# Rows of a two-product expert layer transposed by DMA instead of on TensorE

## The reference

```
x = x + tanh(g_xattn) * expert(layernorm(x), ids)     # every row has one of 4 experts, by its token id
      g = silu(h @ W_e^T); u = h @ W_e^T; y = (g * u) @ W_e   # W_e = ctx[e], 512 x 512, used three times
x = x + tanh(g_ffn) * ffn(layernorm(x))
      base (512 x 512) + shared LoRA + 6 routed LoRA experts (top 2 of a softmax), + bias
```

## Time and profile before

| | us |
|---|---|
| median of 3 runs | 231.8 |
| span of the profiled execution | 229.7 |
| TensorE matmul busy (PE) | 211.8 (92%) |
| TensorE weight load busy (PEld) | 181.7 (79%) |
| VectorE busy | 168.1 (73%) |
| GpSimd busy | 95.4 (42%) |
| ScalarE busy | 77.2 (34%) |

### The profile page before, as it was taken

How to read it: one execution, slowest core, us unless ns; L and a number is a source line. 1 busy time by engine, 2 the same in 40 slices (tenths; PEclk the granted TensorE clock), 3 DMA queues, 4 the chain that set the end, 5 groups by cost and what they waited for, 6 DMA issues and landing times.

```text
span 229.7 us, 4143 instructions
## 1 busy us (share of the span) xinstructions
PE 211.8 (92%) x1203; PEld 181.7 (79%) x1204; DVE 168.1 (73%) x423; ACT 77.2 (34%) x166; POOL 95.4 (42%) x147
## 2 busy tenths in 40 slices
PE   0666999999999999999999999999999999999990
PEld 0325788888888888888888889999999999999990
DVE  5878787777865666555566566768999989999761
ACT  4554334323422122222222216044333344333330
POOL 4887743332223333332100111116666665556742
PEclk9997999999999999999999999999999999999998
DMA  4986082111111111001100000001111111211122
GB/s 126 376 248 212 1 288 72 45 46 46 46 46 46 46 46 40 13 39 46 46 0 0 0 0 0 3 1 47 49 46 46 46 46 46 83 54 46 46 93 91
DMA packets 5994, 15.00 MB, mean 65 GB/s; under 512 B 1073, under 2 KB 1073, under 8 KB 5986
## 3 DMA queue, kind: packets, MB, share of 16 engines
q0 software_dynamic: 2800, 9.18, 12.4%
q1 hardware_dynamic: 2544, 4.21, 5.4%
q10 hardware_dynamic: 642, 1.52, 2.0%
HBM read 10.71 MB, written 4.19 MB: 65 GB/s over the span
## 4 chain that ended last, share of the span: by engine, by line
PE 75%; DVE 10%; issue 6%; POOL 5%; ACT 1%; DMA 1%; POOLq 1%; DVEq 0%
PE z_ps L466 17%; PE y_ps L466 17%; PE y_ps L471 8%; PE z_ps L471 8%; PE hT_ps L476 6%; PE ffn_b L466 4%; PE actT_ps L476 4%; PE ffn_a L466 3%; POOL xg L278 2%; PE ffn_b L471 2%; PE actT_ps L552 2%; DVE bn L845 2%; PE ffn_a L471 2%; POOL lo_onehot L294 2%; DVE hwT L893 1%
## 5 line engine op out<-in xcount | busy, mean ns | idle before, releaser
L269 POOL TENSOR_SCALAR var_eps<-stats 128x1 f32<-128x1 f32 x35 | 7.0, 201 | 107.6 <-DVE stats L757 107.4
L466 PE MATMUL z_ps<-ct_split,hT 128*128 x144 | 39.3, 417 | 1.2 <-ACT hT L349 1.2
L466 PE MATMUL y_ps<-ct_split,actT 128*128 x152 | 39.7, 403 | 0.0
L466 PEld LDWEIGHTS z_ps<-ct_split,hT 128*128 128x128 f32 x144 | 26.7, 195 | 6.5 <-issue 1.5
L466 PEld LDWEIGHTS y_ps<-ct_split,actT 128*128 128x128 f32 x152 | 27.2, 189 | 5.2 <-ACT actT L357 0.2
L357 ACT ACTIVATE actT<-actT_ps 128x512 fp32r<-128x512 f32 x19 | 11.4, 599 | 44.8 <-PE actT_ps L476 44.8
L772 DVE TENSOR_TENSOR act<-z_ps,silu 128x512 f32<-128x512 f32 x18 | 12.5, 692 | 17.8 <-ACT silu L353 17.4
L278 POOL DMA_INDIRECT xg<-x_rows,row_index x19 | 22.4, 1180 | 5.8 <-POOL rstd L272 4.2
L476 PE MATMUL hT_ps<-ident,h 128*128 128x128 f32 x140 | 21.1, 273 | 3.0 <-DVE h L761 3.0
L476 PEld LDWEIGHTS hT_ps<-ident,h 128*128 128x128 f32 x140 | 17.6, 142 | 6.2 <-DVE h L761 3.5
L353 ACT ACTIVATE silu<-z_ps 128x512 f32<-128x512 f32 x18 | 10.8, 599 | 34.3 <-PE z_ps L471 34.3
(11 more groups left out here) (157 smaller groups left out, 419.4 us busy)
## 6 DMA issues: line engine op xcount, KB each, us to landing
ct_stage<-ct SPq DMA_DIRECT2D x4, 1024.0 KB, 8.2
ct_stage<-w_ffn ACTq DMA_DIRECT2D x1, 1260.0 KB
xg<-x_rows,row_index POOLq DMA_INDIRECT x19, 3.6
out<-xg,row_index POOLq DMA_INDIRECT x16
ct_stage<-w_up ACTq DMA_DIRECT2D x1, 226.0 KB
ids_sb<-ids SPq DMA_DIRECT2D x1, 8.0 KB, 1.6
gates_raw<-gates SPq DMA_DIRECT2D x1, 1.0 KB, 2.7
br<-b_router SPq DMA_DIRECT2D x1, 3.0 KB
```

The source lines that it names most:

```text
L466: nc.tensor.matmul(ps, lhs[:, 0, at], rhs(part), start=(k == 0 and part == 0), stop=False)
```

## The change

From item 3 on, the transposes of h leave TensorE. ScalarE rounds h to fp16 (`h_hi`, into the left half of h_split), VectorE writes h - hi as fp16 into the right half (`h_lo`). SP issues one DMA transpose of 128 x 1024 fp16 into hT_half (16 of them, items 3 to 18). When it has landed, ScalarE widens both halves at once to the float32r operand of the product (`widen`, 1024 columns). GpSimd's root gives h times 1024 from item 3 on, and widen takes the factor out again, so that the fp16 remainder stays in range. h_split, hT_half and the operand have two slots each.

The stations are moved: in body q VectorE makes h_lo(q+2) and normalizes item q+3 (before: q+2), and ScalarE makes h_hi(q+2) and widens item q+1, ahead of silu(q). SP no longer forwards landings; VectorE waits for x_landed itself, and since the loops of ScalarE and VectorE are unrolled, each wait names its own semaphore. At body 13 VectorE waits for all gathers; before it did so at body 14. TensorE's loop takes two items in each turn. The sums, the experts' products and the second step are the same.

```diff
+        hTs = (hT, hT_1)
+        h_split = [sb(f"h_split{slot}", [P, 2 * D], F16) for slot in range(2)]
+        hT_half = [sb(f"hT_half{slot}", [P, 2 * KC, P], F16) for slot in range(2)]
...
-            for q in range(ITEMS):
-                sp.wait_ge(x_landed[q], 16)
-                sp.sem_inc(x_ready, 1)
+            for q in range(DMA_FROM, ITEMS):
+                sp.wait_ge(h_lo_ready, q - DMA_FROM + 1)
+                sp.dma_start_transpose(hT_half[q % 2][:], h_split[q % 2][:]).then_inc(hT_landed[q % 2], 16)
...
-                root(n, rstd_ready, 4 + n + 1)
+                root(n, rstd_ready, 4 + n + 1, 1.0 if n < DMA_FROM else 2.0 ** (-2 * H_POWER))
...
+            def h_hi(q):
+                act_e.wait_ge(h_ready, q + 1)
+                if q >= DMA_FROM + 2:
+                    act_e.wait_ge(hT_landed[q % 2], 16 * landings_of(q - 2))
+                nc.scalar.activation(h_split[q % 2][:, 0:D], h[:], ACT.Copy).then_inc(h_hi_ready, 1)
+
+            def widen(q):
+                act_e.wait_ge(hT_landed[q % 2], 16 * landings_of(q))
+                nc.scalar.activation(hTs[q % 2][:].rearrange("p a n -> p (a n)"),
+                                     hT_half[q % 2][:].rearrange("p b t -> p (b t)"), ACT.Copy,
+                                     scale=2.0 ** -H_POWER).then_inc(hT_ready, 1)
...
+            h_hi(3)
+            h_hi(4)
             act_e.wait_ge(w_loaded, 16)
...
+            silu_of(2)
+            widen(3)
+            actT_hi(2)
+            w_hi(0)
+            for q in range(3, ITEMS - 1):
+                if q + 2 < ITEMS:
+                    h_hi(q + 2)
+                widen(q + 1)
+                silu_of(q)
...
+                actT_hi(q)
...
-            with pe.Fori(2, ITEMS - 1) as q:
-                product_z(q)
-                transpose_h(q + 1)
-                product_y(q - 1)
-                transpose_act(q)
...
+            with pe.Fori(DMA_FROM, ITEMS - 2, 2) as q:
+                for turn in range(2):
+                    product_z(q + turn, (DMA_FROM + turn) % 2)
+                    product_y(q + turn - 1)
+                    transpose_act(q + turn)
...
+            def h_lo(q):
+                dve.wait_ge(h_hi_ready, q - DMA_FROM + 1)
+                tt(h_split[q % 2][:, D:], h[:], h_split[q % 2][:, 0:D], ALU.subtract).then_inc(h_lo_ready, 1)
...
+            for q in range(3, ITEMS - 2):
+                if q == EXTRA_AT:
+                    for ahead in range(EXTRA_AT, ITEMS):
+                        dve.wait_ge(x_landed[ahead], 16)
+                h_lo(q + 2)
+                if q + 3 < ITEMS:
+                    item_stats(q + 3)
+                activate(q)
+                if q + 3 < ITEMS:
+                    item_aggregate(q + 3)
+                product_of(q - 1)
...
+                    item_norm(q + 3)
                 actT_lo(q)
```

More of the change, by code:

```diff
@@ L163, in build_block @@
         x_landed = [sem(f"x_landed{q}") for q in range(ITEMS)]
-        x_ready = sem("x_ready")
         first_gathered = sem("first_gathered")
@@ L179, in build_block @@
         hT_done, hT_hi_ready, hT_lo_ready = sem("hT_done"), sem("hT_hi_ready"), sem("hT_lo_ready")
+        h_hi_ready, h_lo_ready, hT_ready = sem("h_hi_ready"), sem("h_lo_ready"), sem("hT_ready")
+        hT_landed = [sem(f"hT_landed{slot}") for slot in range(2)]
         z_done, silu_ready, act_ready = sem("z_done"), sem("silu_ready"), sem("act_ready")
@@ L205, in build_block @@
         CONSTS = 12
+        H_POWER = 10
+        DMA_FROM = 3
         def cols(tensor, position, width=D):
@@ L265, in _, with root @@
             pool.wait_ge(consts_ready, CONSTS)
-            def root(n, done, step):
-                nc.gpsimd.tensor_scalar(var_eps[:], stats[:, 1:2], EPS, 1.0, ALU.add, ALU.mult
+            def root(n, done, step, divisor=1.0):
+                nc.gpsimd.tensor_scalar(var_eps[:], stats[:, 1:2], EPS, divisor, ALU.add, ALU.mult
                                         ).then_inc(pool_step, 1)
@@ L357, in actT_hi, with landings_of @@
                 nc.scalar.activation(actT[:, 0], actT_ps[:], ACT.Copy).then_inc(actT_hi_ready, 1)
[L359 to L362, removed]
+            def landings_of(q):
+                return len(range(q % 2 if q % 2 >= DMA_FROM else DMA_FROM + (q - DMA_FROM) % 2, q + 1, 2))
+            def h_hi(q):
[8 more added lines that the diff above has]
+                                     scale=2.0 ** -H_POWER).then_inc(hT_ready, 1)
             def h2T_hi(l, turn):
@@ L400, in _ @@
             actT_hi(1)
+            h_hi(3)
+            h_hi(4)
             act_e.wait_ge(w_loaded, 16)
[L402 to L408, removed]
+            silu_of(2)
[7 more added lines that the diff above has]
+                silu_of(q)
+                if q < 2 + KC:
+                    w_hi(q - 2)
+                if q == 2 + KC:
+                    act_e.wait_ge(up_loaded, 16)
+                    nc.scalar.activation(up_split[:, 0], up_stage, ACT.Copy).then_inc(w_hi_ready, 1)
+                actT_hi(q)
             silu_of(ITEMS - 1)
@@ L496, in transpose_h, with product_z @@
                 transpose_chunks(hT_ps, h).then_inc(hT_done, 1)
-            def product_z(q):
+            def product_z(q, slot):
                 key = key_of(q)
[L500 to L504, removed]
+                pe.wait_ge(hT_ready, q - DMA_FROM + 1)
+                expert_hi(z_ps, hTs[slot], key)
+                expert_lo(z_ps, hTs[slot], key).then_inc(z_done, 1)
             def product_y(q, key=None, bank_used=True, between=None):
@@ L590, in _ @@
             transpose_act(1)
-            with pe.Fori(2, ITEMS - 1) as q:
-                product_z(q)
-                transpose_h(q + 1)
-                product_y(q - 1)
-                transpose_act(q)
-            product_z(ITEMS - 1)
+            key_2 = key_of(2)
+            pe.wait_ge(ct_lo_ready, S)
+            pe.wait_ge(hT_hi_ready, 3)
+            expert_hi(z_ps, hT, key_2)
+            pe.wait_ge(hT_lo_ready, 3)
+            expert_lo(z_ps, hT, key_2).then_inc(z_done, 1)
+            product_y(1)
+            transpose_act(2)
+            with pe.Fori(DMA_FROM, ITEMS - 2, 2) as q:
[3 more added lines that the diff above has]
+                    transpose_act(q + turn)
+            product_z(ITEMS - 2, (ITEMS - 2) % 2)
+            product_y(ITEMS - 3)
+            transpose_act(ITEMS - 2)
+            product_z(ITEMS - 1, (ITEMS - 1) % 2)
             transpose_h2(0)
@@ L749, in item_stats @@
             def item_stats(q):
[L750 to L753, removed]
+                dve.wait_ge(x_landed[q], 16)
+                if q >= DMA_FROM:
+                    dve.wait_ge(stats_ready, q)
                 nc.vector.bn_stats(bn[:], cols(xg, q)).then_inc(bn_ready, 1)
@@ L766, in hT_lo, with item_aggregate @@
                 tt(to[:, 1], hT_ps[:], to[:, 0].bitcast(F32), ALU.subtract).then_inc(hT_lo_ready, 1)
+            def h_lo(q):
+                dve.wait_ge(h_hi_ready, q - DMA_FROM + 1)
+                tt(h_split[q % 2][:, D:], h[:], h_split[q % 2][:, 0:D], ALU.subtract).then_inc(h_lo_ready, 1)
+            def item_aggregate(q):
+                dve.wait_ge(bn_ready, q + 1)
+                aggregate(stats_ready)
             def activate(q, bn_sem=None, bn_count=0, bank=z_ps):
@@ L813, in _ @@
             actT_lo(0)
[L816 to L826, removed]
-                actT_lo(q)
-            item(1, bank=z_1_ps, first=True)
@@ L830, in _, with product_of @@
[L830 to L841, removed]
+            def product_of(q):
+                if EXTRA_AT <= q < EXTRA_AT + EXTRAS:
+                    dve.wait_ge(x2_ready, q)
+                    add_product(q, target_of(q))
+                else:
+                    add_product(q, q)
@@ new lines, in _ @@
+            item_stats(3)
+            activate(1, bank=z_1_ps)
+            item_aggregate(3)
+            hT_lo(2)
+            gates_of_rows()
+            item_norm(3)
+            add_product(0, 0)
+            actT_lo(1)
+            item_stats(4)
+            h_lo(3)
+            item_aggregate(4)
+            item_norm(4)
+            item_stats(5)
+            activate(2)
+            h_lo(4)
+            item_aggregate(5)
+            add_product(1, 1)
+            item_norm(5)
+            actT_lo(2)
@@ new lines, in _ @@
+            w_lo(0)
+            for q in range(3, ITEMS - 2):
[9 more added lines that the diff above has]
+                product_of(q - 1)
+                if q + 3 < ITEMS:
+                    dve.wait_ge(x2_ready, q)
+                    item_norm(q + 3)
+                actT_lo(q)
+                if q < 2 + KC:
+                    w_lo(q - 2)
+                if q == 2 + KC:
+                    dve.wait_ge(w_hi_ready, KC + 1)
+                    tt(up_split[:, 1], up_stage, up_split[:, 0].bitcast(F32), ALU.subtract).then_inc(w_lo_ready, 1)
@@ L901, in _ @@
             aggregate(stats2_ready)
-            hT_lo(q + 1)
```

## The result

The changed kernel takes 237.12 us (median of 4 runs, 236.02 to 237.93) against 231.62 us before (4 runs): a ratio of 1.0242, 95% interval 1.0216 to 1.0268. It is slower by 5.5 us, where 4.3 us less were forecast; the time lies inside the stated range of 225.7 to 241, on the side of the rival. The profiled execution is the fastest of the four, 236.02 us with a span of 234.3, so the trace has 4.6 us of the 5.5 to explain.

What follows compares the result with a forecast made beforehand. TensorE, busy 92% of the span, was taken to bound the kernel. The terms -8.4 + 3.4 + 0.3 + 0.4 = -4.3 us took the time from 231.8 to 227.5 us, range 225.7 to 241.

Steps and rivals of the forecast that it cites:

- The landing, L = 4.5 us: DMA transpose of h, issue to landing: assumed 4.5 us, hidden in steady items but not at the start.
- The step up from the gather's 3.6 for smaller pieces: DMA transpose: smaller pieces than the gather's 2 KB rows, so landing put somewhat above its 3.6 us, at 4.5.
- The nearest rows: Trace rows used to estimate the landing: 256 KB gather 3.6 us, 8 KB load 1.6, 1 MB load 8.2.
- The term z(3): First DMA item: z(3) starts at 41.8 us where it was 38.39, +3.4 us.
- The path of that term: h_lo(3) ends at 36.2, landing follows at 40.7, widen ends at 41.8, then z(3) starts.
- The slow rival: Landing over 6 us: widen ahead of silu on ScalarE holds TensorE at act's transposes; 240.6 us at 7.1; chance 0.24.
- The clock: TensorE in the item stage: a granted clock below full would be outside all cases; no size given.
- A transpose of h is worth 0.56 us: TensorE, steady items: removal saves 0.56 us each by the loads, 15 x 0.56 = 8.4 us.
- the rival's 0.35: Smaller gain on TensorE: each transpose worth only the matmuls' 0.35 us, 5.3 in all; 230.6 us; chance 0.08.
- Item 13, +0.4: Body 13: h_lo(15) also stands between VectorE's wait for the last gather and act(13), which ends 5.75 into the item.
- the loads on ScalarE and VectorE hidden: Steady items: ScalarE 2.9 us and VectorE about 4.2 us of a 5.85 us item, so no cost.
- the sum of the prediction: Transposes removed -8.4, z(3) +3.4, the item after it +0.3, item 13 +0.4; z(3)'s floor was +2.1.

Runs made afterwards that it cites:

- first experiment: Changed kernel with the 113-row w_up load cut into 112 rows and 1 row; 229.47 us, 0.9907 of the kernel before.
- the experiments from item 4 on: Changed kernel with the DMA transposes starting at item 4 instead of item 3, in several variants; 226.31 to 232.33 us.
- the fifth: Changed kernel with DMA transposes from item 4 on, item 3 transposed on TensorE, w_up load whole; 232.33 us, 1.0042 of the kernel before.
- seventh: Changed kernel with DMA transposes from item 4 on, w_up load cut, wait for all gathers at body 14; 227.03 us, 0.981 of the kernel before.
- eighth: Changed kernel, DMA transposes still from item 3, with w_up load cut and wait for all gathers at body 14; 229.25 us, 0.9908.
- the control: Kernel before the change, with only its w_up load cut into 112 rows and 1 row; 231.94 us, ratio 1.002.
- ninth: The seventh kernel with silu(3) ahead of widen(4) in ScalarE's queue, in body 3 alone; 226.31 us, 0.9777 of the kernel before.
- tenth: The ninth kernel with silu(q) ahead of widen(q+1) in every body; 226.4 us, 0.9781 of the kernel before.
- third: Changed kernel, w_up load whole, with an added same-size DMA transpose of zeros ahead of item 3's; 237.79 us, 1.0269 of the kernel before.
- sixth: Changed kernel with DMA transposes from item 4 on and the w_up load cut into 112 rows and 1 row; 227.41 us, 0.984.

## Why the prediction was wrong

- **The landing, L = 4.5 us.** This step failed, and in an unforeseen way: there was no one L. Undisturbed it is 3.1 us (first experiment), shorter than assumed and than the gather's 3.6; beside the w_up load it is 9.8. The step up from the gather's 3.6 for smaller pieces was wrong in its sign: the pieces are small (the queue that carries them has 19440 packets instead of 2544, which is 1056 for each transpose, and 4.2 MB more, so about 250 bytes in each), and the landing is still no later. The nearest rows bounded the size of the transfer. What they left out was what else ran at 36 us, which the windows of the kernel before show (share 0.07 until 44 us). The term z(3) was put at +3.4 and is +8.9; with the load cut it is 41.06 - 38.39 = +2.7. The path of that term was right: with 9.8 in the place of 4.5 it gives z(3) at 47.1, and it came at 47.30.
- **The slow rival** was given 0.24, and its place in all bodies: a time of about 240 us for a landing above 6. The sign was its, the mechanism was not: no steady item waited. Apart from the three small delays of the account, the loss lies in one late landing and the slow item behind it, and it came to TensorE through z(3) itself. That the time fell into the stated range is luck: the range reached that far for a rival in which about every second steady item waits.
- **The clock.** The prediction called a fall outside of all its cases. It costs about 1.6 us in item 3 (7.61 against 5.95): in the first experiment z(3) takes 4.21 us from its first load to that of y (45.27 - 41.06) where a steady one takes 2.65, and the rest of the item is as long as a steady one. With the first DMA transpose one item later and the load cut, it is gone.
- **A transpose of h is worth 0.56 us.** Mis-sized: an item fell by 0.46 us, so 15 x 0.46 = 6.9 instead of 8.4. In the kernel before, in the item of the earlier trace rows, the last four matmuls of y:

```profile
107.46 0.88 PEld L471 LDWEIGHTS y_ps<-ct_split,actT 128*128 128x128 f32 x4
...
107.69 1.08 PE L471 MATMUL y_ps<-ct_split,actT 128*128 x4
```

  The two sides of TensorE agree. By the loads 0.56 us go and 0.10 come back, since the eight loads of y go from 105.73 to 107.46 (1.73 us) behind transposes and from 87.67 to 89.50 (1.83) behind the matmuls of z. By the matmuls 0.35 go and another 0.10 with them, since the eight of y take 1.94 before (107.69 - 105.75) and 1.84 after (89.73 - 87.89). The measured value lies halfway between the forecast's 0.56 and the rival's 0.35, and neither holds. Why the 0.10 is there isn't shown.
- **Item 13, +0.4.** The place was right (in body 13 VectorE waits 1.59 us for the last gather), the size is 0.7, and the way another. Act(13) ends at 113.45 + 0.67 = 114.12, 5.29 us into the item where 5.75 was forecast, and its transposes load at 114.23, just in rhythm. But then come 0.69 us before z(14) that the profile puts to issue:

```profile
113.45 0.67 DVE L815 TENSOR_TENSOR act<-z_ps,silu 128x512 f32<-128x512 f32 x1
...
114.23 0.59 PEld L503 LDWEIGHTS actT_ps<-ident,act 128*128 128x128 f32 x4
...
115.50 1.68 PEld L493 LDWEIGHTS z_ps<-ct_split,hT 128*128 128x128 f32 x8 [0.69 <-issue]
```

  What stands there in the queue is the load of the expert's number. My reading is that it is hidden only while TensorE's sequencer is well ahead of the matmuls; when the sequencer itself has waited for act, the load lies open. A gap of the same kind, 0.65 to 1.01 us (0.35 once, in the fifth), stands behind each late act in the experiments from item 4 on. That the later wait for the gathers removes it at item 13 is shown (seventh and eighth); no kernel without the load of the number was run, so that load as the cause is argued, not shown.
- **Right:** the loads on ScalarE and VectorE hidden, h_lo 0.69 us (0.66 taken), widen 1.05, silu(2) at 38.39 (38.6), the norm of item 4 at 37.27 (37.4), no wait in steady items. Carried with L = 3.1 the sum of the prediction is -8.4 + 2.1 + 0.1 + 0.4 = -5.8; the first experiment's span is 1.7 below the one before, and the difference of 4.1 is the 0.1 us of fifteen items (1.5), the clock (1.6), z(3) (0.6) and the short stalls of items 4, 6 and 13.

## What to carry to other kernels

Before a transfer is put on the critical path, look at the DMA share in the windows where it will run: a share near 1/16 over many microseconds fits one engine working alone. Here it cost nothing (the control, 1.002 with the load cut) until a transpose had to land beside it. A load with an awkward number of rows (113) can be cut in an even part and a rest, at no cost that showed here. And when work is handed to a latency path, start it where the first one has a whole item to land in, with nothing that is due earlier queued behind its consumer: that order, the cut and the later wait together gave 226.3 us, 0.9777 of the kernel before, out of a change that by itself was 2.4% slower.

## What the runs showed of the hardware

- A DMA transpose of 128 x 1024 fp16 within SBUF took 3.11 us from issue to the start of what waited for it (first experiment); landings were 3.0 to 3.6 us in the ninth and tenth. The 256 KB gather takes 3.4 to 3.9 to landing (medians of the runs). Beside the uncut 226 KB load of 113 rows the transpose took 9.7 to 11.9 us, 6.1 beside the rest of it, and 8.2 at the start beside a 1 MB load (third).
- Where the transpose and the 113-row load meet, the DMA share is above 1 at a low rate, in the changed kernel:

```profile
42.00:44.00 2.00, 0.00 (x0) 0.00 (x0) 0.00 (x0) 0.00 (x0) 0.77 (x1) 0.50 1.33 56
```

  My reading is that packets which wait for each other count as busy: at a share of 1.02 the same engines moved 396 GB/s in the kernel before (30 to 32 us).
- The granted clock fell to half (1.2 GHz) after TensorE had been idle with one short burst from 37.9 to 41.1 us (first experiment), and stayed full where it had been idle for 0.9 and 0.45 us (sixth).
- Four 128-column transposes took 0.56 us of TensorE's loads, and their removal gave 0.46 us (5.95 against 6.41 us for an item).
